# Six 512-column matmuls put ahead of the third tile in three node stages of a four-layer graph network kernel

## The chip, the cores and the metric

The kernel runs as one program on one core of a Trainium2 chip. The metric is the device time of an execution in microseconds, the median of several runs. A core has five engines with instruction streams of their own: TensorE (PE in the rows, its weight loads PEld), VectorE (DVE), ScalarE (ACT), GpSimd (POOL) and SyncE (SP, which here only issues DMAs). They wait for one another through semaphores. TensorE has two clock levels, 2.4 and 1.2 GHz; the profile calls the granted share of full speed PEclk, 1.00 and 0.50.

## The reference

The network has 6250 nodes with 160 features each (64 scalars, 32 vectors of three components) and 100000 edges, sorted by their destination node. Four layers each normalise the nodes, map them, gather rows by the edges' source, multiply by edge weights, sum the messages at the destination and map the sums. What matters here:

```python
h = jnp.maximum(_layernorm(x, axis=-1), 0.0)
# layer 0, nodes: self map and source map, times a node attribute
out_s = xs @ Ws * (a / np.sqrt(xs.shape[1]))[:, None]
out_v = jnp.einsum('nuc,uw->nwc', xv, Wv) * (a / np.sqrt(xv.shape[1]))[:, None, None]
# layer 3, nodes: two source maps and two self maps, each times an attribute
s_s, s_v = (ssa + ssc, sva + svc)
x1s, x1v = (l1a_s + l1c_s, l1a_v + l1c_v)
# layer 2, the end: message sums to nodes, four heads
agg = jax.ops.segment_sum(alpha * h, dst, num_segments=n)
out = node + jnp.concatenate([agg_s @ Wps,
      jnp.einsum('ncx,cd->ndx', agg_v, Wpv).reshape(n, CV * 3)], axis=-1)
```

## The kernel before, in words

The nodes stay in SBUF in x, as 49 tiles of 128 nodes by 160 features, in float32. For this input the kernel takes the path `streamed()` (L2481). Its stages follow one another, most of them with a barrier between: the setup; the node pass of layer 0 (L2514); the edge streams of layers 0 and 1, which hold the node passes of layers 1 and 2 in their tails; the attention pass, the softmax and the gathering of the messages of layer 2 (L2269); `post_l2` (L2359), which maps the sums of messages to nodes; the node pass of layer 3 (L2470); and the edge stream of layer 3, which ends with the store. The change touches the node pass as it is called for layers 0 and 3, and `post_l2`. The branch `general()` calls them too, and isn't taken here.

`node_pass` (L351) first computes the normalisation of all tiles on VectorE, with one square root on ScalarE. Then each of the 49 tiles goes through ScalarE (L434: scale, bias and relu into `tile`), TensorE (L458 and L459: two transposes into the bank `ps_t`), ScalarE (L443, L444: copies to `tile_T`), TensorE (L464: the map of the 64 scalars, L465: the map of the 96 vector components; a float32 matmul appears as two instructions) and VectorE (`finish_l0`, L500 to L503, or `finish_l3`, L520 to L530). SyncE stores the rows for the edge stream (L406). TensorE's order is written by hand: in its step i it transposes tile i and then maps tile i-1. It waits for `copied` before a transpose, for `tile_ready` before a map, and for `fin` of the tile two before the one that it maps, since each of `ps_t`, `ps_s` and `ps_v` has two banks; six of the eight banks are in use. Layer 0 maps to 128 scalar and 192 vector columns, layer 3 to 256 and 384, and its `finish_l3` has eight instructions where `finish_l0` has four.

`post_l2` has one map for each tile: ScalarE copies 84 rows of sums (L2405), TensorE multiplies them with two blocks of 322 columns (L2417, four instructions of 84 rows in all), and VectorE adds a small constant to the denominators (L2445), takes reciprocals (L2447) and adds four products to the tile (L2453). It has four slots of two banks, so all eight banks are in use.

`steps` (L70) writes the first few steps of a stage out one by one (i is then a Python integer) and the others as a loop whose waits and addresses come from registers.

`warm_up(bank)` (L533) issues six matmuls of the identity with the first 512 columns of x into a bank that nobody reads. Four places call it before the change (L637, L906, L1909, L2314): in the edge streams, in the attention pass and in the gathering of the messages, each at the fifth step of the stage.

Of the kernel before, what the change touches and what calls it, by code (L numbers as in the profile page):

```python
# [22 lines left out]
P = 128  # L23
# [22 lines left out]
def build(nc, A, out):  # L46
# [9 lines left out]
    def at_least(eng, sem, value):  # L56

        if isinstance(value, int) and value <= 0:
            return
        eng.wait_ge(sem, value)  # L60
# [9 lines left out]
    def steps(eng, n, lag, emit, warm=4, unroll=2):  # L70


        for i in range(warm):
            emit(i, i % unroll, i // unroll)
        turns = (n - warm) // unroll
        with eng.Fori(0, turns) as j:
            for k in range(unroll):
                emit(j * unroll + (warm + k), (warm + k) % unroll, j + (warm + k) // unroll)
        for i in range(warm + turns * unroll, n + lag):
            emit(i, i % unroll, i // unroll)  # L80

    def live(i, n):
        return not isinstance(i, int) or 0 <= i < n

    def back(s, r, lag, unroll=2):

        return (s - lag) % unroll, r + (s - lag) // unroll
# [16 lines left out]
    def sbuf(ctx, name, shape, dt=F32):  # L104
        return ctx.enter_context(nc.sbuf_tensor(side[0] + name, shape, dt))

    def psum(ctx, name, shape):
        return ctx.enter_context(nc.psum_tensor(side[0] + name, shape, F32))
# [3 lines left out]
    def sem(ctx, name):  # L112
        layer_sems.append(nc.alloc_semaphore(side[0] + name))
        return layer_sems[-1]
# [20 lines left out]
    with whole:  # L135
        x = sbuf(whole, "x", [P, NT * FEAT])
        y4 = sbuf(whole, "y4", [P, NG * TG * 4])
        sums_T = sbuf(whole, "sums_T", [P, 4 * COLS])
        dst_rel = sbuf(whole, "dst_rel", [P, NG * TG])
# [5 lines left out]
        ident = sbuf(whole, "ident", [P, P])  # L145
# [205 lines left out]
        def node_pass(tag, scalar_maps, vector_maps, tables, finish, n_fin, coefs=(), gamma=None):  # L351
# [6 lines left out]
            with ExitStack() as ctx:  # L358
# [9 lines left out]
                ps_t = [psum(ctx, f"{tag}_ps_t{s}", [P, 512]) for s in range(2)]  # L368
                ps_s = [psum(ctx, f"{tag}_ps_s{s}", [P, 512]) for s in range(2)]
                ps_v = [psum(ctx, f"{tag}_ps_v{s}", [P, 512]) for s in range(2)]  # L370
                zeroed = sem(ctx, f"{tag}_zeroed")
                cleared = sem(ctx, f"{tag}_cleared")
                w_loaded = sem(ctx, f"{tag}_w_loaded")
# [11 lines left out]
                with nc.Block() as block:  # L385

                    @block.sync
                    def _(sp):
                        for n, w in enumerate(scalar_maps):
                            sp.dma_start(w_s[:, n * SC:(n + 1) * SC], A[w]).then_inc(w_loaded, 16)  # L390
                        sp.wait_ge(zeroed, 1)

                        for n, w in enumerate(vector_maps):
                            for c in range(XYZ):
                                at = n * VF + c * VC
                                sp.dma_start(w_v[c:VF:XYZ, at:at + VC], A[w]).then_inc(w_loaded, 16)
                        if gamma:
                            sp.dma_start(gam[0:SC, 0:1], A[gamma[0]]).then_inc(w_loaded, 16)
                            sp.dma_start(gam[0:SC, 1:2], A[gamma[1]]).then_inc(w_loaded, 16)
                            for c in range(XYZ):  # L400
                                sp.dma_start(gam[c:VF:XYZ, 2:3], A[gamma[2]]).then_inc(w_loaded, 16)

                        def store(i, s, r):
                            sp.wait_ge(fin, (i + 1) * n_fin)
                            for k in range(n_tab):
                                sp.dma_start(tables[k][ds(i * P, P), :], rows[s][k][:, :]).then_inc(stored[s], 16)  # L406

                        steps(sp, NT, 0, store, unroll=U)
                        for s in range(U):
                            sp.wait_ge(stored[s], 16 * n_tab * len(range(s, NT, U)))  # L410
                        sp.wait_ge(cleared, 1)
# [36 lines left out]
                    @block.tensor  # L448
                    def _(pe):
                        pe.wait_ge(w_loaded, 16 * n_w)  # L450
                        if gamma:
                            pe.wait_ge(w_ready, 1)

                        def step(i, s, r):
                            if live(i, NT):
                                at_least(pe, copied, (i + 1) * (2 if gamma else 1))
                                at_least(pe, tile_ready, 2 * (i - 1))
                                nc.tensor.transpose(ps_t[s][0:VF, P:2 * P], tile[s][:, SC:FEAT], ident[:, :])  # L458
                                nc.tensor.transpose(ps_t[s][0:SC, 0:P], tile[s][:, 0:SC], ident[:, :]).then_inc(turned, 1)  # L459
                            if live(i - 1, NT):  # L460
                                s1, _ = back(s, r, 1)
                                at_least(pe, tile_ready, 2 * i)
                                at_least(pe, fin, (i - 2) * n_fin)
                                nc.tensor.matmul(ps_s[s1][:, 0:ns], tile_T[s1][0:SC, 0:P], w_s[:, :])  # L464
                                nc.tensor.matmul(ps_v[s1][:, 0:nv], tile_T[s1][0:VF, P:2 * P], w_v[:, :]).then_inc(mapped, 1)  # L465

                        steps(pe, NT, 1, step)
# [62 lines left out]
            nc.vector.scalar_tensor_tensor(xv_at(t), by_component(ps_v[:, 3 * VF:4 * VF]), c1, xv_at(t),  # L530
                                           ALU.mult, ALU.add).then_inc(fin, 1)

        def warm_up(bank):  # L533


            for _ in range(6):
                nc.tensor.matmul(bank[:, 0:512], ident[:, :], x[:, 0:512])  # L537


        def edge_pass(tag, first, rows_of, edge_T, w_in, w_mid, w_out, act_fn, scales):  # L540
# [1818 lines left out]
        def post_l2():  # L2359
# [5 lines left out]
            with ExitStack() as ctx:  # L2365
# [6 lines left out]
                ps = [psum(ctx, f"l2_post_ps{s}", [P, 2, 512]) for s in range(U)]  # L2372
# [10 lines left out]
                with nc.Block() as block:  # L2383

                    @block.sync
                    def _(sp):
                        sp.wait_ge(zeroed, 1)
                        for b in range(2):
                            for k in range(2):
                                h, at = 2 * b + k, k * HF  # L2390
                                sp.dma_start(w_all[at:at + HS, b, 0:SC], A["L2_gnn_Wps"][h * HS:(h + 1) * HS, :]).then_inc(w_loaded, 16)
                                for c in range(XYZ):
                                    lo = at + HS + c * HV
                                    sp.dma_start(w_all[lo:lo + HV, b, SC + c * VC:SC + (c + 1) * VC],
                                                 A["L2_gnn_Wpv"][h * HV:(h + 1) * HV, :]).then_inc(w_loaded, 16)
# [13 lines left out]
                    @block.tensor  # L2409
                    def _(pe):  # L2410
                        pe.wait_ge(w_made, 12)

                        def step(i, s, r):
                            at_least(pe, copied, i + 1)
                            at_least(pe, fin, (i - 3) * 4)
                            for b in range(2):
                                ins = nc.tensor.matmul(ps[s][:, b, 0:2 * FEAT + 2], sums[s][:, b, :], w[:, b, :])  # L2417
                            ins.then_inc(mapped, 1)

                        steps(pe, NT, 0, step, unroll=U)  # L2420
# [49 lines left out]
        def layer_3_nodes():  # L2470
            import math
            c_self = math.sin(math.pi / 8)
            node_pass("l3", ["L3_gnn_Ws_l1_a", "L3_gnn_Ws_l1_c", "L3_gnn_Ws_sc_a", "L3_gnn_Ws_sc_c"],
                      ["L3_gnn_Wv_l1_a", "L3_gnn_Wv_l1_c", "L3_gnn_Wv_sc_a", "L3_gnn_Wv_sc_c"], [table[4]], finish_l3, 8,
                      [(0, 1.0), (1, 1.0), (0, c_self), (1, c_self)])
# [17 lines left out]
        def general():  # L2493

            all_windows(EDGE_WIN, lambda tag, first: edge_pass(tag + "l0", first, *L0))
            post_l0()
            node_pass("l1", ["L1_gnn_W1_s", "L1_gnn_W_sc_s"], ["L1_gnn_W1_v", "L1_gnn_W_sc_v"], [table[1], self_rows], finish_l1, 4,
                      [(0, SC ** -0.5), (0, VC ** -0.5)])
            all_windows(EDGE_WIN, lambda tag, first: edge_pass(tag + "l1", first, *L1))
            post_l1()  # L2500
            node_pass("l2", ["L2_gnn_Ws_src", "L2_gnn_Ws_dst"], ["L2_gnn_Wv_src", "L2_gnn_Wv_dst"], [table[2], table[3]], finish_l2, 4,
                      gamma=("L2_gnn_gamma_s", "L2_gnn_beta_s", "L2_gnn_gamma_v"))
            attention_pass()
            softmax_pass()
            spread_exps()
            all_windows(SUM_WIN, gather_messages)
            post_l2()
            layer_3_nodes()
            all_windows(EDGE_WIN, lambda tag, first: edge_pass(tag + "l3", first, *L3))
            post_l3()  # L2510
            store_x()
# [67 lines left out]
```

## Time and profile before

| | us |
|---|---|
| median of 3 runs | 7133.47 (7131.9 to 7139.69) |
| the profiled execution's span | 7132.6 |
| PE busy | 6597.2 (92%) |
| DVE busy | 4139.3 (58%) |
| POOL busy | 4496.1 (63%) |
| layer 0's node pass, from its first transpose | 58.9 to about 162 |
| `post_l2`, from its first matmul | 5621.6 to about 5732 |
| layer 3's node pass, from its first transpose | 5756.0 to about 5913 |

The span is one execution from the first to the last instruction, taken by the profiler; it lies within 1 us of the median. Busy is the time in which an engine worked; the end of a matmul is modelled, and matmuls overlap in the array, so a PE that is busy throughout can still be at half its clock or at work that fills it poorly. PEclk in a row of stretches is the mean granted share. The three stages together are some 370 us of the span.

### The profile page before, as it was taken

To read this page: it belongs to the slowest core of one execution; us is meant where nothing else is said; L and a number is where in the kernel's file an instruction comes from. 1 tells how busy PE (TensorE), PEld (TensorE's weight loads), DVE (VectorE), ACT (ScalarE), POOL (GpSimd) and SP (SyncE) were. 2 spreads that over 40 slices of the span, in tenths; PEclk is the share of its full clock that TensorE was granted. 3 is DMA by queue.
4 is the path that set the end of the run, shared out by engine and by line. 5 is a ranking of instruction groups with operands and counts; after the bars stand their busy time and mean duration, and the time that the engine had idled before them with its cause. 6 is when DMAs were issued, how large, how long until landed. Compare 5 with 4: busy or idle time off the path is not lost. (4 is left out here: it accounts for less than half of the span.)

```text
span 7132.6 us, 185025 instructions
## 1 busy us (share of the span) xinstructions
PE 6597.2 (92%) x57917; PEld 5320.6 (75%) x57917; DVE 4139.3 (58%) x11420; ACT 2382.5 (33%) x6454; POOL 4496.1 (63%) x4226
## 2 busy tenths in 40 slices
PE   6999999899999969999999999999838889999999
PEld 3788888677877757887787787777727636878787
DVE  4555555344444447777777777777658863333333
ACT  2122222112112136666666666666500021111111
POOL 1677777577777757788788878878500015666665
PEclk9999999899999978899889889888869758999999
DMA  1444444354445434444444444444337303444443
GB/s 60 114 121 125 122 123 125 97 131 124 127 125 130 126 66 79 79 83 83 81 81 85 81 82 83 81 81 83 78 91 203 90 19 102 116 117 115 114 117 97
DMA packets 810369, 719.46 MB, mean 101 GB/s; under 512 B 248938, under 2 KB 682074, under 8 KB 809602
## 3 DMA queue, kind: packets, MB, share of 16 engines
q0 software_dynamic: 263424, 321.38, 22.4%
q1 hardware_dynamic: 546818, 396.43, 19.8%
q8 instruction: 75, 1.23, 0.1%
q14 instruction: 52, 0.43, 0.0%
HBM read 557.59 MB, written 159.75 MB: 101 GB/s over the span
## 5 line engine op out<-in xcount | busy, mean ns | idle before, releaser
L892 POOL DMA_INDIRECT l_edge_g<-node_table,l_edge_idx x2352 | 2271.0, 966 | 1292.7 <-issue 937.9
L939 PEld LDWEIGHTS l_edge_win_ps<-l_edge_hot,l_edge_prod 128*128 128x128 f32 (+2 forms) x14112 | 1309.6, 149 | 212.2 <-issue 171.3
L939 PE MATMUL l_edge_win_ps<-l_edge_hot,l_edge_prod 128*128 128x40 f32 (+2 forms) x14112 | 1438.3, 255 | 29.8 <-DVE sums_T L752 22.0
L1857 POOL DMA_INDIRECT att_g<-node_table,att_ends x784 | 1241.1, 1583 | 238.8 <-issue 238.8
L957 ACT ACTIVATE l_edge_h<-l_edge_h_ps 128x256 f32<-128x256 f32 (+1 forms) x784 | 342.8, 437 | 2755.0 <-PE l_edge_h_ps L913 2540.9
L1850 POOL DMA_INDIRECT att_g<-node_table,att_ends x784 | 791.4, 1009 | 301.4 <-issue 272.8
L993 DVE TENSOR_TENSOR l_edge_prod<-l_edge_w_ps,l_edge_g 128x512 f32<-128x512 f32 x588 | 405.6, 690 | 958.0 <-PE l_edge_w_ps L920 810.3
L1877 PE MATMUL att_turn<-ident,sums_T 128*128 128x128 f32 (+1 forms) x4704 | 774.4, 309 | 29.7 <-ACT sums_T L1962 23.2
L1962 ACT ACTIVATE sums_T<-att_turn 128x512 f32<-128x512 f32 (+1 forms) x1176 | 666.1, 592 | 214.6 <-PE att_turn L1877 206.9
L1877 PEld LDWEIGHTS att_turn<-ident,sums_T 128*128 128x128 f32 (+1 forms) x4704 | 572.2, 153 | 204.7 <-issue 120.3
L920 PEld LDWEIGHTS l_edge_w_ps<-l_edge_wo,l_edge_h 64*128 64x128 f32 (+1 forms) x4704 | 503.4, 190 | 287.6 <-issue 285.2
L752 DVE TENSOR_TENSOR sums_T<-sums_T,l_edge_win_ps 128x160 f32 x588 | 189.2, 322 | 878.7 <-PE l_edge_win_ps L943 705.8
L920 PE MATMUL l_edge_w_ps<-l_edge_wo,l_edge_h 64*128 64x192 f32 (+1 forms) x4704 | 679.7, 351 | 0.0
L943 PE MATMUL l_edge_win_ps<-l_edge_hot,l_edge_prod 128*32 128x40 f32 x14112 | 620.6, 204 | 0.0
L997 DVE TENSOR_TENSOR l_edge_prod<-l_edge_w_ps,l_edge_g 128x384 f32<-128x384 f32 x1176 | 594.5, 547 | 0.0
L943 PEld LDWEIGHTS l_edge_win_ps<-l_edge_hot,l_edge_prod 128*32 128x32 f32 x14112 | 568.2, 115 | 0.0
L913 PE MATMUL l_edge_h_ps<-l_edge_ea,l_edge_wi 16*128 16x256 f32 (+1 forms) x1176 | 497.3, 503 | 51.4 <-DMA l_edge_ea<-in_edge_attr_T 49.5
L1934 PEld LDWEIGHTS att_o<-att_w_o1v,sums_T 128*128 128x128 f32 x1568 | 287.9, 216 | 109.9 <-issue 92.8
L1952 ACT ACTIVATE att_gy<-att_g,y 128x160 f32<-128x160 f32 x784 | 270.2, 416 | 252.6 <-DMA att_g<-node_table,att_ends 252.4
L1917 PE MATMUL att_o<-att_w_o2s,sums_T 96*128 96x64 f32 x1568 | 333.7, 297 | 10.7 <-ACT sums_T L1962 1.5
L1935 PE MATMUL att_o<-att_w_o1v,sums_T 128*128 128x64 f32 x1568 | 338.7, 302 | 0.0
L1919 PE MATMUL att_o<-att_w_o2v,sums_T 128*128 128x64 f32 x1568 | 329.6, 295 | 0.0
(271 smaller groups left out, 10179.5 us busy)
## 6 DMA issues: line engine op xcount, KB each, us to landing
l_edge_hot<-hot_tiles SPq DMA_DIRECT2D x392, 320.0 KB
hot_tiles<-l_edge_hot SPq DMA_DIRECT2D x196, 320.0 KB, 2.3
l_messages<-att_rows SPq DMA_DIRECT2D x196, 320.0 KB
sum_msg<-l_messages SPq DMA_DIRECT2D x196, 320.0 KB, 3.6
l_edge_g<-node_table,l_edge_idx POOLq DMA_INDIRECT x2352
att_g<-node_table,att_ends POOLq DMA_INDIRECT x1568
att_ea<-in_edge_attr_T SPq DMA_DIRECT2D x196, 64.0 KB
l_scores<-att_score SPq DMA_DIRECT2D x784, 2.0 KB
```

What stands on the lines that cost most here:

```text
L892: pool.indirect_dma_start(g[s][:, t, :], None, rows_of, bass.IndirectOffsetOnAxis(idx[s][:, t:t + 1], 0)).then_inc(fetched[s], 16)
L913: nc.tensor.matmul(h_ps[0:HALVES * hid, 0:HC], wi[:, :], ea[s0][:, :]).then_inc(hidden[0], 1)
L920: ins = nc.tensor.matmul(w_ps[s1][:, m * (TG // HALVES) + n, 0:wn], h[last][s1][m * hid:(m + 1) * hid, n * P:(n + 1) * P], wo[m * hid:(m + ...
L939: nc.tensor.matmul(at, q[:, t, lo:lo + width], to[:, t, kinds, :], start=t == 0, stop=t == TG - 1)
L943: ins = nc.tensor.matmul(win[SC:MID, 2 * W:3 * W], q[:, t, lo:lo + VC], to[:, t, 1 + c, :], start=c + t == 0, stop=c + t == XYZ + TG - 2)
L957: nc.scalar.activation(h[n][s % 2][:, :], h_ps[0:HALVES * hid, 0:HC], act_fn, scale=scales[n]).then_inc(active[n], 1)
L993: nc.vector.tensor_tensor(halves[:, :, :, 0:SC], w[:, :, 0:2 * SC].rearrange("p t (n f) -> p t n f", n=2), rows[:, :, 0:SC].unsqueeze(2).t ...
L997: ins = nc.vector.tensor_tensor(q[:, :, lo:lo + VF].rearrange("p t (c u) -> p t c u", c=XYZ), w[:, :, VS + n * VC:VS + (n + 1) * VC].unsqu ...
L1850: pool.indirect_dma_start(g[s][:, t, :], None, table[2], bass.IndirectOffsetOnAxis(ends[s][:, t:t + 1], 0)).then_inc(fetched[s], 16)
L1857: pool.indirect_dma_start(g[s1][:, t, :], None, table[3], bass.IndirectOffsetOnAxis(ends[s1][:, TG + t:TG + t + 1], 0), compute_op=ALU.add ...
L1877: ins = nc.tensor.transpose(turn[bank][0:width, t * P:(t + 1) * P], f[:, t, at:at + width], ident[:, :])
L1962: nc.scalar.activation(feat_T[n][0:width, part, :], turn[bank][0:width, :], ACT.Copy).then_inc(count, 1)
```

## The change

At the third tile (i == 2, which is in the steps written out) TensorE first issues the six matmuls, and then its instructions of that step. In the node pass they go into a seventh bank, `spare_ps`, allocated for them; in `post_l2` into the first bank of slot 3, before that slot's first real matmul, which overwrites it. The 512 moving columns come from `dst_rel`, which is constant after the setup, and no longer from x, which VectorE is writing at that point. No wait, no DMA and no instruction of another engine is added or moved, and the four earlier calls stay as they were.

```diff
+                spare_ps = psum(ctx, f"{tag}_spare_ps", [P, 512])
...
                         def step(i, s, r):
+                            if isinstance(i, int) and i == 2:
+                                warm_up(spare_ps, dst_rel)
                             if live(i, NT):
...
-        def warm_up(bank):
+        def warm_up(bank, moving=x):
             for _ in range(6):
-                nc.tensor.matmul(bank[:, 0:512], ident[:, :], x[:, 0:512])
+                nc.tensor.matmul(bank[:, 0:512], ident[:, :], moving[:, 0:512])
...
                         def step(i, s, r):
+                            if isinstance(i, int) and i == 2:
+                                warm_up(ps[3][:, 0, :], dst_rel)
                             at_least(pe, copied, i + 1)
```

## Rows read from the trace of the kernel before

**Rows 1.** The page: TensorE's granted clock in 40 slices of the span, in tenths.

```profile
PEclk9999999899999978899889889888869758999999
```

**Rows 2.** Stretches: length, busy time (instructions) of each engine, PEclk, DMA share, GB/s.

```profile
58.00:162.00 104.00, 102.52 (x294) 66.48 (x294) 46.45 (x195) 43.65 (x147) 0.00 (x0) 1.00 0.12 37
5622.00:5727.00 105.00, 105.00 (x196) 65.50 (x195) 84.48 (x281) 18.76 (x45) 0.00 (x0) 0.50 0.00 0
5756.00:5912.00 156.00, 154.79 (x294) 67.29 (x294) 92.70 (x389) 43.02 (x146) 0.00 (x0) 0.50 0.08 25
```

**Rows 3.** Groups of the two node passes: count, busy us, mean ns, idle before.

```profile
L458 PE MATMUL l_ps_t<-ident,l_tile 128*96 128x128 f32 x49 | 20.6, 421 | 37.9 <-ACT l_tile L434 37.9
...
L458 PE MATMUL l_ps_t<-ident,l_tile 128*96 128x128 f32 x49 | 20.6, 421 | 28.9 <-ACT l_tile L434 28.9
```

**Rows 4.** A stretch of the attention pass, and its transposes of 128 columns.

```profile
2833.00:2840.50 7.50, 5.70 (x47) 5.06 (x45) 4.56 (x16) 3.49 (x10) 5.98 (x6) 1.00 0.51 90
...
L1877 PE MATMUL att_turn<-ident,sums_T 128*128 128x128 f32 x8 | 1.0, 273 | 0.0
```

**Rows 5.** Timeline of layer 0's node pass: start us, length, engine, instruction, idle before.

```profile
63.93 0.28 DVE L500 TENSOR_SCALAR l_rows<-l_ps_s,l_coef 128x64 f32<-128x64 f32 x1 [1.03 <-PE l_ps_v L465]
64.25 0.79 PE L464 MATMUL l_ps_s<-l_w_s,l_tile_T 64*128 64x128 f32 x2
64.55 0.33 DVE L503 SCALAR_TENSOR_TENSOR x<-l_ps_v,l_coef,x 128x96 f32<-128x96 f32 x1
66.33 0.79 PE L464 MATMUL l_ps_s<-l_w_s,l_tile_T 64*128 64x128 f32 x2
```

**Rows 6.** Timeline of layer 3's node pass, within the loop.

```profile
5769.79 1.22 PE L464 MATMUL l_ps_s<-l_w_s,l_tile_T 64*128 64x256 f32 x2
...
5772.94 0.28 DVE L520 TENSOR_SCALAR l_temp<-l_ps_s,l_coef 128x64 f32<-128x64 f32 x1 [1.52 <-PE l_ps_v L465]
5772.94 1.22 PE L464 MATMUL l_ps_s<-l_w_s,l_tile_T 64*128 64x256 f32 x2
5773.05 0.27 ACT L443 ACTIVATE l_tile_T<-l_ps_t 64x128 f32<-64x128 f32 x1 [2.23 <-PE l_ps_t L459]
5773.59 0.52 ACT L434 ACTIVATE l_tile<-x,norm 128x160 f32 x1
5774.04 0.28 DVE L526 SCALAR_TENSOR_TENSOR l_rows<-l_ps_s,l_coef,l_temp 128x64 f32<-128x64 f32 x1 [0.15 <-DVE x L523]
5774.66 0.34 DVE L530 SCALAR_TENSOR_TENSOR x<-l_ps_v,l_coef,x 128x96 f32 x1
```

**Rows 7.** Timeline of `post_l2`: its start, its third tile on VectorE, and its end.

```profile
5621.57 4.66 PE L2417 MATMUL l_post_ps<-l_post_w,l_post_sums 84*128 84x322 f32 x8 [9.89 <-DVE l_post_w L2440]
...
5628.42 0.16 DVE L2445 TENSOR_SCALAR l_post_inv<-l_post_ps 128x4 f32<-128x4 f32 x1
...
5718.33 8.79 PE L2417 MATMUL l_post_ps<-l_post_w,l_post_sums 84*128 84x322 f32 x16
...
5727.57 0.15 DVE L2445 TENSOR_SCALAR l_post_inv<-l_post_ps 128x4 f32<-128x4 f32 x1
...
5729.73 0.15 DVE L2445 TENSOR_SCALAR l_post_inv<-l_post_ps 128x4 f32<-128x4 f32 x1
```

**Rows 8.** Instructions of L537 in the gathering of the messages: duration min/median/max, first and last start.

```profile
L537 PE MATMUL sum_spare_ps<-x,ident x12: 592/592/648, 5295.6 to 5300.4; 128*128 128x512 f32 x12
```

**Rows 9.** Stretches as in rows 2: the gathering of the messages, from its start.

```profile
5285.00:5290.00 5.00, 0.31 (x3) 0.34 (x3) 1.68 (x5) 0.00 (x0) 3.18 (x1) 0.50 0.00 0
5290.00:5295.00 5.00, 5.00 (x40) 5.00 (x40) 2.76 (x9) 0.00 (x0) 0.00 (x0) 0.53 0.53 135
5295.00:5300.00 5.00, 5.00 (x22) 2.61 (x21) 2.35 (x7) 0.00 (x0) 0.00 (x0) 1.00 0.69 186
5300.00:5610.00 310.00, 268.48 (x3075) 244.80 (x3073) 276.30 (x764) 0.00 (x0) 0.00 (x0) 1.00 0.75 198
```

**Rows 10.** Stretches as in rows 2: the edge stream of layer 0 around a drop.

```profile
400.00:403.40 3.40, 1.99 (x16) 1.76 (x15) 1.83 (x4) 1.70 (x4) 2.49 (x4) 1.00 0.54 154
403.40:406.80 3.40, 3.40 (x40) 3.00 (x37) 0.00 (x0) 0.00 (x0) 2.48 (x4) 0.50 0.30 71
```

## The prediction, made before the changed kernel was run

> **What bounds the kernel now.** I read the page's clock line first [rows 1]. TensorE is at nine tenths of full clock or more over most of the span and lowest around slice 32, where `post_l2` and layer 3's node pass lie. The stretches [rows 2] say it sharply: `post_l2` runs 105 us and layer 3's node pass 156 us at a granted 0.50, the 1.2 GHz level, though PE is busy for 105.00 and 154.79 us of them. So in these stages TensorE isn't starved: it works all the time at half clock.
>
> For layer 0's node pass the same view prints 1.00. I don't believe it. The groups [rows 3] give the 128-column transpose L458 421 ns in layer 0 and 421 ns in layer 3, where the clock is 0.50; the 128-column transpose L1877 in a stretch at 1.00 takes 273 ns [rows 4]. Equal forms with equal durations have equal clocks, so layer 0's pass is at 1.2 GHz too, and its printed 1.00 is a clock that no record covers. The only term of mine that rests on this is layer 0's.
>
> Next, who waits for whom. In layer 0 a tile takes 66.33-64.25=2.08 us on PE, and VectorE starts its tile after 1.03 us of waiting for L465 [rows 5]. In layer 3 a tile takes 5772.94-5769.79=3.15 us, with waits of 1.52 us by VectorE and 2.23 us by ScalarE, both for PE [rows 6]. PE sets the pace of both passes. `post_l2` is different: PE's last matmul ends at 5718.33+8.79=5727.12, and VectorE still has two tiles to do; it starts them 5729.73-5727.57=2.16 us apart with nothing left to wait for. From its third tile to the last it took (5729.73-5628.42)/46=2.20 us a tile, while PE produced one each 2.15 us (5727.12-5621.57=105.55 us for 49). VectorE is the bound there, by a hair [rows 7].
>
> **The block by itself.** Six float32 matmuls are twelve instructions. At 1.00 the last of twelve starts 4.8 us after the first and lasts 0.59 [rows 8], about 5.3 us in all. That is the lower end, if the clock were up from the start. At 1.2 GHz all the way it would be near twice that, 10.5 us: the upper end. Between them: in the gathering of the messages PE goes from idle to busy at about 5290 and the clock is up some 5 us later: the mean of 0.53 in 5290 to 5295 leaves 0.3 us at 1.00 [rows 9]. With 5 us at half speed 2.5 us of full-speed work are done, and 5.3-2.5=2.8 remain: 7.8 us a block. PE has nothing else to do meanwhile, and everybody waits for it.
>
> Will the block raise the clock at all? No row shows that: the twelve of rows 8 ran at full level already, and so did the others of L537, by their 592 ns. For it: the bursts after which the clock rose had 128-row matmuls back to back [rows 9], as the block has. The node passes and `post_l2` have matmuls of 64, 96 and 84 rows, and stay at 0.50 however busy they are [rows 2].
>
> The Trainium skill has a rule that speaks against the change's need (TensorE: Matmul & The Clock Gate, "Why this matters for your kernels"): keep TensorE continuously busy and it is granted its full clock. By that rule `post_l2`, busy 105.00 us of 105.00, would be at 1.00, all three stages would be fast already, and the change would only add three blocks, about 16 us. The row says 0.50 [rows 2], so the measurement decides against the rule here: how long PE is busy is not enough, and what it is busy with counts.
>
> **Layer 0's node pass.** 47 tiles follow the block. At full clock, PE needs at least half of 2.08, 1.04 us, and at most 2.08*273/421=1.35 us, if everything shrinks only as the whole transpose does [rows 3, 4]. VectorE needs 64.55+0.33-63.93=0.95 us [rows 5] plus the 0.15 us that an own completion costs it in the loop [rows 6], 1.10. ScalarE needs 5773.59+0.52-5773.05=1.06 us [rows 6], and again up to 0.15. All three come close together; I take 1.20 us, near the middle. The gain is 47*(2.08-1.20)=41.4 us (34 to 49), the block costs 7.8, and the net is -34 us, if the clock stays up. PE would then be at work nearly all the time, so I take it that it does.
>
> **Layer 3's node pass.** PE would need 3.15/2=1.58 us at least, 3.15*273/421=2.04 at most. VectorE needs 5774.66+0.34-5772.94=2.06 us and 0.15 for its wait for itself: 2.21 us [rows 6]. So VectorE becomes the bound, and PE then idles in every tile. The gain is at most 47*(3.15-2.21)=44 us, less 7.8: -36 us. But does the clock stay? The nearest rows: the edge stream lost its 1.00 right behind a stretch in which PE was busy for 1.99 of 3.40 us, and the gathering kept it for 310 us with 268 us busy, all in 128-row matmuls [rows 9, 10]. Layer 3's PE would be busy about 1.6 to 2.0 of 2.21 us, in 64- and 96-row matmuls for three quarters of it. That lies between, and nearer to the loser: I expect the clock to fall back after roughly a quarter of the tiles, 12. Then the gain is 12*0.94=11 us, and with the block -3 us; range +8 to -36.
>
> **`post_l2`.** VectorE already runs at its own pace of 2.16 to 2.20 us, so a faster PE brings nothing. The block starts when PE is done with tile 1, about 5625.9 (4 x 1.07 us behind 5621.57), and ends at 5633.7; tile 2's matmuls take 1.1 us at full clock, so VectorE starts that tile near 5634.9 and not at 5628.42: +6.5 us. At the block's ends: +4 and, as VectorE's lag at the end absorbs some, +8.
>
> The Trainium skill states for holding the clock that gaps between bursts of matmuls are what loses it (same page, "HAM oscillation — how this bites in real kernels"). Layer 3's PE would have only short gaps, so by that rule the clock would stay up: that is the first rival below. Rows 10 agree that waiting loses it, but show no gap that long beforehand.
>
> Nothing else moves: no DMA, no wait and no other engine's instruction is added, and each stage ends in a barrier, before which PE idles anyhow. Sum: -34-3+6.5=-31 us on the profiled 7132.6, thus about 7102; the median is 0.9 us above the span: 7102.5.
>
> **The rivals.** (1) The clock rises and stays in both node passes: -34-36+6.5=-63.5, 7070 us. For it: short gaps only. Against it: PE idles a fifth of the time or more, in low-row matmuls. (2) Slower: the blocks run, but the passes can't hold the level, or it never rises. The block is PE's only new work, and it's exposed in all three places: 7.8+7.8+6.5=+22 if the clock drops right behind each, 10.5+10.5+8=+29 if it never rises: 7155 to 7162. For it: the passes' own matmuls stay at 0.50 for 100 us and more [rows 2], and no row shows a block that lifted anything. It decides once fewer than some 9 tiles of layer 0 (7.8/0.88) run at full clock. (3) Both passes lose the level on the way: layer 0 halfway (-21+8=-13), layer 3 soon (+2), `post_l2` +6.5: 7129 us, within the noise at the edge. (4) Layer 0's printed 1.00 is true; then its block is pure loss, 5.3 us, and the sum is near +9: 7142. The 421 ns speak against that.
>
> **How the numbers follow.** Forecast 0.42, rival 1 0.24, rival 2 0.17, rival 3 0.12, rival 4 0.05. What a measurement can tell from no change is about 0.2%, 14 us. Forecast and rival 1 are faster: 0.66, and a third of rival 3 lands beyond 14 us: 0.70. The rest of rival 3 and most of rival 4 are the same: 0.12. Slower is rival 2 and the remainder: 0.18. The forecast's own range, from its pace bounds (1.10 to 1.35 us in layer 0: -5, +7) and from layer 3's +8 to -20, is 7080 to 7121. Eight in ten must take in rival 1 and the near end of rival 2: 7062 to 7155.
>
> **What would show it.** In the changed trace: twelve instructions of L537 near 62 us, 5626 us and 5760 us, each block 7 to 9 us long, the later ones of a block at 592 ns; L458 at about 270 ns behind the block in layer 0, with tiles 1.1 to 1.3 us apart; granted 1.00 in the first 20 to 40 us behind the block of layer 3, L520 starting each 2.2 us there, and 3.15 us apart once the clock is back at 0.50; in `post_l2` the same 2.16 to 2.20 us a tile on VectorE, whatever the clock. The prediction is wrong if L458 stays at 421 ns in layer 0, if layer 3's whole pass stays at 1.00, or if `post_l2` gets shorter.

## The result, and the profile after

The changed kernel takes 7091.07 us, the median of 6 runs (7077.21 to 7106.26), against 7132.68 (7118.78 to 7139.69) for the kernel before. The ratio is 0.9945, with a 95% interval of 0.9928 to 0.9963. A second measurement of the same pair gave 0.9950 (0.9928 to 0.9972). So it is faster by about half a per cent, 39 to 42 us, where 31 were forecast. One profile used below, that of the kernel without a block in `post_l2`, is of an execution in the slow state; what is read from its stages stands in other runs too.

The profiled execution of the changed kernel has a span of 7081.9 us, 50.7 under that of before, more than the medians differ by. Cutting both traces at the first and the last instruction of each stage shows where this lies:

| us | before | changed | difference | forecast |
|---|---|---|---|---|
| layer 0's node pass, first transpose to last update | 103.6 | 67.0 | -36.6 | -34 |
| edge streams of layers 0 and 1 | 2400.1 | 2399.3 | -0.8 | 0 |
| attention pass and softmax | 2727.0 | 2708.8 | -18.2 | 0 |
| gathering of the messages | 331.9 | 332.2 | +0.3 | 0 |
| `post_l2`, first matmul to last update | 110.2 | 115.8 | +5.6 | +6.5 |
| layer 3's node pass | 156.9 | 154.8 | -2.1 | -3 |
| edge stream of layer 3 | 1219.7 | 1220.6 | +0.9 | 0 |

The three stages that the change touches give -33.1 us. The other large entry, the attention pass, has the same code in both kernels; the experiments come back to it. The table leaves out the 24 us between `post_l2` and layer 3's first transpose, which are equal in both.

First the blocks. Instructions of L540 (L537 before) in the changed kernel; columns as in [rows 8]:

```profile
L540 PE MATMUL l_spare_ps<-dst_rel,ident x24: 592/592/1061, 61.8 to 5717.1; 128*128 128x512 f32 x24
L540 PE MATMUL sum_spare_ps<-x,ident x12: 592/592/648, 5240.6 to 5245.4; 128*128 128x512 f32 x12
L540 PE MATMUL l_post_ps<-dst_rel,ident x12: 592/592/1061, 5570.9 to 5577.5; 128*128 128x512 f32 x12
```

The new blocks begin at 1061 ns an instruction and end at 592, where the old block in the gathering never was slower than 648: the new ones meet the engine at its lower level and lift it. The timeline of layer 0's block and what follows:

```profile
61.77 7.18 PE L540 MATMUL l_spare_ps<-dst_rel,ident 128*128 128x512 f32 x12
...
65.19 0.34 PEld L540 LDWEIGHTS l_spare_ps<-dst_rel,ident 128*128 128x128 f32 x1 [0.52 <-issue]
65.79 0.19 PEld L540 LDWEIGHTS l_spare_ps<-dst_rel,ident 128*128 128x128 f32 x1 [0.27 <-issue]
...
70.15 0.28 DVE L503 TENSOR_SCALAR l_rows<-l_ps_s,l_coef 128x64 f32<-128x64 f32 x1 [7.08 <-PE l_ps_v L468]
71.31 0.28 DVE L503 TENSOR_SCALAR l_rows<-l_ps_s,l_coef 128x64 f32<-128x64 f32 x1 [0.20 <-PE l_ps_v L468]
72.47 0.28 DVE L503 TENSOR_SCALAR l_rows<-l_ps_s,l_coef 128x64 f32<-128x64 f32 x1 [0.20 <-PE l_ps_v L468]
```

The weight loads fall from 0.34 to 0.19 us at about 65.5, some 3.8 us into the block. VectorE waits 7.08 us for it, and then works a tile each 1.16 us instead of 2.08 [rows 5], with 0.20 of waiting left. The transposes behind the block, against 421 ns in [rows 3]:

```profile
L461 PE MATMUL l_ps_t<-ident,l_tile 128*96 128x128 f32 x47 | 12.9, 274 | 0.0
```

The granted clock in stretches, with columns as in [rows 2]. The first is layer 0 behind the rise. The next three are `post_l2` ahead of its rise, at full level, and afterwards, and the last three are the same for layer 3.

```profile
65.50:126.00 60.50, 59.32 (x294) 39.56 (x293) 45.87 (x192) 41.12 (x139) 0.00 (x0) 1.00 0.21 62
5570.90:5574.60 3.70, 3.70 (x6) 1.59 (x5) 2.08 (x7) 0.42 (x1) 0.00 (x0) 0.50 0.00 0
5574.60:5588.30 13.70, 12.08 (x39) 6.90 (x39) 7.69 (x27) 2.91 (x7) 0.00 (x0) 1.00 0.00 0
5588.30:5676.00 87.70, 87.34 (x159) 46.10 (x157) 71.77 (x239) 14.99 (x36) 0.00 (x0) 0.50 0.00 0
5710.20:5714.60 4.40, 4.40 (x7) 1.76 (x6) 1.91 (x8) 0.00 (x0) 0.00 (x0) 0.50 0.06 19
5714.60:5735.10 20.50, 17.90 (x60) 8.28 (x58) 14.01 (x59) 8.05 (x27) 0.00 (x0) 1.00 0.08 24
5735.10:5859.00 123.90, 123.90 (x235) 53.89 (x234) 75.77 (x318) 33.04 (x113) 0.00 (x0) 0.50 0.09 26
```

Layer 0 keeps 1.00 to its end. `post_l2` loses it after 13.7 us and layer 3 after 20.5 us. Layer 3's timeline around the loss, against [rows 6]:

```profile
5731.45 0.27 PE L461 MATMUL l_ps_t<-ident,l_tile 128*96 128x128 f32 x1
5732.28 0.70 PE L467 MATMUL l_ps_s<-l_w_s,l_tile_T 64*128 64x256 f32 x2 [0.44 <-DVE x L533]
5733.65 0.28 PE L461 MATMUL l_ps_t<-ident,l_tile 128*96 128x128 f32 x1
5734.48 0.70 PE L467 MATMUL l_ps_s<-l_w_s,l_tile_T 64*128 64x256 f32 x2 [0.44 <-DVE x L533]
5736.54 0.42 PE L461 MATMUL l_ps_t<-ident,l_tile 128*96 128x128 f32 x1
5737.11 1.22 PE L467 MATMUL l_ps_s<-l_w_s,l_tile_T 64*128 64x256 f32 x2
```

Before it PE waits 0.44 us a tile for VectorE (L533), with tiles 2.20 us apart; behind it the matmuls are long again and VectorE waits for PE. Right behind the block, while VectorE was still catching up, the first tiles were 1.69 us apart. And `post_l2`'s end, against [rows 7]:

```profile
5669.52 6.94 PE L2422 MATMUL l_post_ps<-l_post_w,l_post_sums 84*128 84x322 f32 x12
...
5673.74 0.15 DVE L2450 TENSOR_SCALAR l_post_inv<-l_post_ps 128x4 f32<-128x4 f32 x1
5675.90 0.15 DVE L2450 TENSOR_SCALAR l_post_inv<-l_post_ps 128x4 f32<-128x4 f32 x1
5678.06 0.15 DVE L2450 TENSOR_SCALAR l_post_inv<-l_post_ps 128x4 f32<-128x4 f32 x1
5680.22 0.15 DVE L2450 TENSOR_SCALAR l_post_inv<-l_post_ps 128x4 f32<-128x4 f32 x1
```

VectorE's tiles are 2.16 us apart as before, with PE two tiles ahead.

### The profile page after: what moved, and what is told of

It reads as the page before. It is cut to its first block and busy times, and to the rows that moved or that the text cites. A ratio compares the mean times of both kernels' runs of the same rounds, so it can differ in the third digit from the quotient of the medians.

```text
span 7081.9 us, 185097 instructions
## 1 busy us (share of the span) xinstructions
PE 6533.2 (92%) x57953; PEld 5266.3 (74%) x57953; DVE 4141.2 (58%) x11420; ACT 2379.8 (34%) x6454; POOL 4494.5 (63%) x4226
## 5 line engine op out<-in xcount | busy, mean ns | idle before, releaser
L1938 PE MATMUL att_o<-att_w_o1v,sums_T 128*128 128x64 f32 x1568 | 339.3, 302 | 0.0
L1920 PE MATMUL att_o<-att_w_o2s,sums_T 96*128 96x64 f32 x1568 | 329.1, 294 | 10.7 <-ACT sums_T L1965 1.5
L1937 PE MATMUL att_o<-att_w_o1v,sums_T 128*128 128x64 f32 x1568 | 326.1, 293 | 0.0
```

The source lines that it names most:

```text
L1937: nc.tensor.matmul(o1[:, t, Q:PV + VC], feat_T[0][:, 1, e], w_o1v[0][:, :])
```

## The experiments

The first four were measured in a series of measurements in which the kernel before takes 9442.66 us (median of 23 runs) and not 7133. The edge streams of layers 0 and 1 take 3544 us there against 2400, and the attention pass about 3400 against 2727. In the stages studied here unchanged code takes the same time in both (`post_l2` 110.3 and 110.2 us, layer 3's pass 156.9 and 156.9), so these runs are read by their stages. Why the other stages are slower is open. It isn't shown to be the chip: this series and a later one, in which the kernel before takes 7151, carry the same chip number. Of all runs below only the first two and the last two have several executions behind their totals; the others are one execution each, and only their stages are read.

**Only layer 0's block.**

```diff
-                            if isinstance(i, int) and i == 2:
+                            if isinstance(i, int) and i == 2 and tag == "l0":
                                 warm_up(spare_ps, dst_rel)
...
-                            if isinstance(i, int) and i == 2:
-                                warm_up(ps[3][:, 0, :], dst_rel)
```

> Only layer 0's block stays. My theory (each stage's gain is its own): layer 0's pass, from its first transpose to the end of its last update, takes 67 us instead of 103, `post_l2` 110 and layer 3's pass 157 us as before the change; the whole is 36 us under the kernel before, near 7096. Rival (the three blocks together do something for the stages between, where the changed kernel's profile is 18 us shorter than I can account for): the middle, from layer 0's pass to `post_l2`, comes back to the 5459 us of before and the gain is under 36 us.

Measured: layer 0's pass 67.8 us, `post_l2` 110.3, layer 3's pass 156.9. Each block acts on its own stage alone. The whole is 0.9986 of the kernel before (0.9948 to 1.0023): in this series the other stages vary too much for 36 us to be seen in the total, so the rival on the middle stays open here.

**No block in `post_l2`.** The second half of the diff above.

> The blocks of layers 0 and 3 stay, that of `post_l2` goes. My theory (`post_l2` is bound by VectorE, so its block only costs): `post_l2` back from 115.8 to 110.2 us, layers 0 and 3 at 67 and about 155 us, the whole 5 to 6 us under the changed kernel, near 7086. Rival (a faster PE does help `post_l2`): it stays at 116 us or gets longer than 110, and the whole is no better than the changed kernel.

Measured: 66.3, 110.3 and 155.7 us; 0.9951 of the kernel before (0.9914 to 0.9987). `post_l2` is back at its old length, as in the five later runs without its block (110.2 to 110.3 us). The block cost 5.5 us and gave nothing.

**Blocks of 64 rows.**

```diff
-                nc.tensor.matmul(bank[:, 0:512], ident[:, :], moving[:, 0:512])
+                nc.tensor.matmul(bank[:, 0:512], ident[0:rows, :], moving[0:rows, 0:512])
```

with rows=64 in the three new calls (`rows` is a new argument, 128 by default).

> The three blocks use only 64 rows of the identity and of the moving tile, the same number of instructions and columns. Theory A (what PE is busy with counts, and low-row matmuls don't lift the clock): the granted clock stays at 0.50 in all three stages, each block takes about 10.3 us, layer 0's pass 114 us, layer 3's 167, `post_l2` 118 to 120, some 29 us over the kernel before. Rival (long dense columns count, whatever their rows): blocks of about 7 us and layer 0's pass at 67 us as in the changed kernel.

Measured: 114.3, 121.1 and 167.6 us in the three stages, each 10.7 to 10.9 us over the kernel before (a little more than expected in `post_l2`). The rows of its blocks:

```profile
L540 PE MATMUL l_spare_ps<-dst_rel,ident x24: 1057/1057/1219, 61.9 to 7561.1; 64*128 64x512 f32 x24
L540 PE MATMUL l_post_ps<-dst_rel,ident x12: 1057/1057/1219, 7406.9 to 7416.4; 64*128 64x512 f32 x12
```

None is faster than 1057 ns. The same instructions and columns, at the same pace to begin with, lift the clock with 128 rows and don't with 64. This is rival 2 of the prediction made to happen; it is the rows that keep the change from it. Each row of the identity brings one non-zero weight, and no run separates the number of rows from that of such weights.

**Blocks of three matmuls.** `warm_up(..., 3)` in the three new calls.

> Three matmuls (six instructions) a block instead of six, 5.1 us at half clock. In the changed kernel the clock rose 3.7 to 4.3 us into each block, at its fifth or sixth instruction. Theory (the first half of the block does the lifting, the rest only costs): the clock rises in layer 0 and layer 3, layer 0's pass takes about 64.5 us. Rival (where the block falls against the chip's own timing decides, and a short one can miss): at least one of the three stages stays at 0.50 throughout, layer 0's pass then at 108 us.

Measured: 64.8, 112.7 and 147.7 us. The clock rose in all three stages, and each block cost less: in `post_l2` 2.4 us instead of 5.5. Layer 3 kept it 27.3 us this time, which is part of its gain. The rival isn't excluded by this: in layer 0 the clock rose 4.3 us into a block of 4.9, and in other runs with long blocks up to 5.4 us into one. In the five stages with a short block it rose each time.

The next five ran in series in which the kernel before takes 7151 us (one run) and 7132 (median of 14).

**A 128-row matmul in every tile of layer 3.** No block in `post_l2`, and behind the transposes of the node pass:

```diff
+                                if tag in ("l3",) and not (isinstance(i, int) and i < 2):
+                                    nc.tensor.matmul(spare_ps[:, 0:192], ident[0:128, :], dst_rel[0:128, 0:192])
```

> Blocks in layers 0 and 3 (none in `post_l2`), and in every tile of layer 3's pass one more unread matmul between its transposes and its maps, 192 columns with 128 rows of the identity. Theory (the clock fell in layer 3 because PE, waiting for VectorE, did too little in its rows; more rows at work hold it): 1.00 to the end of the pass, tiles at VectorE's 2.2 us, the pass about 115 us instead of 155 to 157. Rival (the clock is held only for a time after a block, whatever follows; layer 0 just ended in time, 61 us after the rise): it falls after 20 to 60 us, and the tiles then cost 3.15+0.8 us, the pass 150 us or more.

Measured: layer 3's pass takes 117.5 us, with its clock up to the end of its matmuls.

**The same with 32 rows.** `ident[0:32, :], dst_rel[0:32, 0:192]`.

> As the run before, but the added matmul of each tile takes only 32 rows of the identity, with the same columns and so the same time on PE. Theory A (rows at work count): hardly more than none, the clock falls within some 10 to 30 us of the rise, and the pass gets longer than the 157 us of the kernel before, about 175 to 185. Theory B (idle gaps of PE count, rows don't): the gaps are filled as with 128 rows, the clock stays, about 115 us.

Measured: 118.4 us, with the clock up until 0.8 us before the end of the last matmul. My theory A as I had put it failed: 32 rows are enough. That left two readings, that rows count and little was missing, or that only PE's gaps or columns count. The run with a single row tells them apart.

**The same with one row.** `ident[0:1, :], dst_rel[0:1, 0:192]`.

> As the two runs with an added matmul per tile in layer 3, with a single row of the identity: the same columns and the same time on PE, and next to nothing in its rows. Theory A (rows at work count; 32 of them were just enough): the clock falls within 10 to 40 us of the rise and the pass takes about 175 to 185 us. Theory B (PE's idle gaps or its moving columns count, rows don't): 1.00 to the end and 117 to 119 us, as with 32 and 128 rows.

Measured: the clock falls 13.7 us after its rise, as theory A says, and the pass takes 198.9 us, longer than its 175 to 185. The stretches behind the blocks, first with 128 rows:

```profile
5730.40:5837.00 106.60, 98.53 (x376) 53.08 (x376) 91.70 (x384) 40.81 (x138) 0.00 (x0) 0.99 0.12 36
```

With 32 rows:

```profile
5707.30:5815.00 107.70, 104.74 (x376) 52.76 (x376) 91.75 (x384) 40.57 (x137) 0.00 (x0) 0.98 0.12 36
```

With one row, ahead of the fall and after it:

```profile
5741.40:5751.00 9.60, 9.60 (x36) 4.90 (x35) 6.49 (x28) 4.21 (x15) 0.00 (x0) 1.00 0.08 26
5751.00:5925.00 174.00, 174.00 (x341) 79.73 (x340) 81.66 (x343) 36.86 (x125) 0.00 (x0) 0.50 0.07 20
```

(The 0.99 and 0.98 come from the last microseconds, as the pass ends.) The one-row run has PE busy for 9.60 of 9.60 us and loses the clock; with 128 rows PE is busy for 98.53 of 106.60 and keeps it. Busy time doesn't order these runs, rows do. The cleanest pair is 32 rows against one: with both, tiles are 2.20 to 2.21 us apart at full level and the added matmul has the same columns. At 0.50 a tile then costs 4.09 us, the 3.15 of before and 0.94 for the added matmul, so this filler costs most where it fails: 42 us over the kernel before in this stage.

**Less work on VectorE in layer 3.** `finish_l3` without its four updates of x, so that the self maps are missing from the output; no block in `post_l2`. `finish_l3` then increments `fin` four times a tile and not eight, and the call says so (not shown).

```diff
-            nc.vector.scalar_tensor_tensor(xs_at(t), ps_s[:, 2 * SC:3 * SC], c0, xs_at(t), ALU.mult, ALU.add).then_inc(fin, 1)
...
-            dve.wait_ge(fin, k + 4)
+            dve.wait_ge(fin, k + 2)
```

> Blocks in layers 0 and 3; `finish_l3` leaves out its four additions to x (the self maps of layer 3 are missing from the output), so VectorE needs 1.2 to 1.4 us a tile and no longer 2.2. Theory (VectorE's pace makes PE idle and so loses the clock): PE is the bound at the 1.69 us a tile that it had right behind the block, 1.00 to the end, the pass about 91 us. Rival (64- and 96-row matmuls can't hold it in layer 3 whatever the pace): the clock falls as in the changed kernel and the pass takes over 140 us.

Measured: 92.5 us, tiles 1.69 us apart throughout, and in its stretch:

```profile
5723.80:5805.00 81.20, 80.43 (x284) 39.16 (x283) 48.49 (x191) 40.97 (x139) 0.00 (x0) 1.00 0.15 47
```

The same 64- and 96-row matmuls hold the clock when VectorE doesn't thin them out. So in the changed kernel layer 3 lost its clock because its matmuls came each 2.2 us and not each 1.7.

**The clock held in `post_l2`.** The changed kernel with, ahead of each tile's maps:

```diff
+                            if not (isinstance(i, int) and i < 3):
+                                nc.tensor.matmul(ps[s][:, 0, 0:192], ident[:, :], dst_rel[:, 0:192])
```

> The changed kernel with one more unread 128-row matmul of 192 columns ahead of each tile's maps in `post_l2`, so that the clock is held there. Theory (VectorE bounds `post_l2`): 1.00 to the end of the stage and still 115 to 116 us, VectorE's tiles 2.16 to 2.20 us apart. Rival (PE's pace matters): with the clock up the stage falls below the 110 us of the kernel before.

Measured: 116.0 us. The stretch and the maps in it:

```profile
5615.00:5714.00 99.00, 78.62 (x282) 48.75 (x280) 79.71 (x266) 17.92 (x43) 0.00 (x0) 0.98 0.00 0
```

```profile
L2424 PE MATMUL l_post_ps<-l_post_w,l_post_sums 84*128 84x322 f32 x172 | 54.9, 441 | 0.0
```

The maps take 441 ns instead of 742, the clock is up for nearly the whole stage, and its length is what it was with the block alone. (The 0.98 holds one fall of 3.4 us, at 5643.) VectorE is the bound of `post_l2` at either level.

**The version these point to, and the changed kernel beside it.** Blocks of three matmuls in layers 0 and 3, none in `post_l2`, and in each tile of layer 3 `nc.tensor.matmul(spare_ps[:, 0:64], ident[:, :], dst_rel[:, 0:64])`.

> What the runs so far point to: blocks of three matmuls in layers 0 and 3, none in `post_l2`, and in layer 3 one unread 128-row matmul of 64 columns a tile. Expected: layer 0's pass 65 us, `post_l2` 110, layer 3's pass 113 to 116 with 1.00 to its end; together 81 us under the kernel before, near 7052, and about 40 us under the changed kernel. Rival (64 columns are too few, or the short block misses the lift in one of the passes): layer 3's pass over 145 us, and no more than 50 us under the kernel before.

> The changed kernel again, beside the version above. Stage by stage as before: 67, 115.8 and about 155 us; the whole 33 us under the kernel before (the sum of the three stages), if the further 18 us that its first profile showed in the attention pass are spread of that pass and not of the change. Rival (the change shortens the attention pass too): 45 to 55 us under the kernel before.

Measured, on the same chip: the new version 7052.64 us (median of 6), 0.9883 of the kernel before (0.9856 to 0.9910), with 64.8, 110.3 and 114.0 us in the three stages, in sum 81.6 under before. The changed kernel 7093.57 (median of 9), 0.9950, with 66.2, 115.8 and 154.7, in sum 34.0 under. Both totals follow from their stages within their intervals. Layer 3 in the new version:

```profile
5718.00:5824.00 106.00, 91.16 (x376) 52.89 (x374) 91.70 (x384) 40.61 (x137) 0.00 (x0) 1.00 0.12 36
```

**The attention pass.** Its code is the same in all kernels. In the profiles outside the slower series it took 2727.0 (before), 2708.8 (changed) and, in the order of the runs above, with the changed kernel's second profile last, 2730.4, 2706.8, 2728.4, 2719.2, 2742.5, 2708.1 and 2712.8 us. Its stretches in before, in the changed kernel, and in the longest one:

```profile
2562.60:5289.60 2727.00, 2460.39 (x17679) 2047.29 (x17679) 1957.67 (x5520) 1636.20 (x4536) 2043.31 (x1570) 0.85 0.41 79
```

```profile
2525.40:5234.20 2708.80, 2435.32 (x17679) 2024.84 (x17679) 1957.78 (x5520) 1633.67 (x4536) 2043.39 (x1570) 0.86 0.41 80
```

```profile
2529.00:5271.00 2742.00, 2477.03 (x17679) 2059.94 (x17679) 1959.04 (x5518) 1634.98 (x4536) 2049.68 (x1570) 0.84 0.41 79
```

In these three it is longer where less clock was granted; over all nine that holds only roughly. Kernels that contain the change had both nearly the shortest and the longest. I take the 18.2 us of the first pair for this spread. It isn't shown: there is only one such profile of the kernel before, and the interval of the second measurement reaches 51 us, 17 more than its stages give, so that a part of the 18 us may still belong to the change.

## Why the prediction was right, point by point

- **Layer 0 ran at 1.2 GHz in spite of its printed 1.00: right.** Equal forms had 421 ns before and 274 behind the block. The changed trace prints 1.00 for its first microseconds too, where L540 takes 1061 ns.
- **The block lifts the clock: right,** which no row of before showed. The reason given, 128-row matmuls, was the right one: 64 rows don't.
- **The block's price: 7.8 us forecast, 7.1 of waiting measured in layer 0.** The rise came 3.7 to 4.3 us into the block in this trace. Over all runs in which a block lifted the clock it came 1.6 to 5.4 us into it, so that the forecast's 5 lies inside, and a block of six took between 6.3 and 8.0 us.
- **Layer 0's pace: 1.20 forecast, 1.16 to 1.17 measured,** and with the price above this makes some -36 of the measured -36.6, for a forecast of -34. That the clock stays up was forecast from PE being at work nearly all the time. It did stay, but the one-row run shows that busy time alone doesn't hold it, so the reason given was incomplete.
- **Layer 3's pace at full level: 2.21 forecast, 2.20 measured,** VectorE being the bound. The fall after a quarter of the tiles, 12: it came after nine at full level, and -3 became -2.1. The 12 was placed between two rows and not computed, and in the five layer 3 passes with a block and nothing added the level lasted 17 to 27 us, so how near it came is in part luck. What I had weighed was mainly PE's idling; the run with one row shows that idling is not the measure and that the rows in use count. In the changed kernel the two go together, so the forecast held for a reason that was only half named.
- **`post_l2`: +6.5 forecast, +5.6 measured,** and bound by VectorE with the clock held as well.
- **Rival 1** (the clock stays in both passes) would have come true with one 32-row matmul of 192 columns more a tile, or with less work on VectorE: the forecast was right by a small margin, and 0.24 was not too much for it. The Trainium skill's rule that gaps are what loses the clock (TensorE: Matmul & The Clock Gate, "HAM oscillation — how this bites in real kernels") is not borne out by the one-row run, where PE was busy for 9.60 of 9.60 us ahead of the fall.
- **What was left out:** the sum took the rest of the kernel as fixed. The attention pass alone spreads by 36 us between single executions, from 2706.8 to 2742.5. Of the 39 to 42 us of the medians the three stages explain 33 to 34; the rest is within the intervals and its cause isn't shown.

## What to carry to other kernels

A stage in which TensorE sets the pace and is granted half its clock, although it is busy throughout, can be lifted by a few dense full-row matmuls that nobody reads; check first that no other engine's pace lies just below, since then the block only costs (here 5.6 us). In every lift seen here the clock rose while the block still ran, at most 5.4 us into it; whether a block that ends sooner lifts it isn't shown. Holding the clock is a question apart from raising it: where another engine becomes the bound, a small full-row matmul in each tile, put where TensorE would wait anyway, held it and, with the shorter block, turned 2 us of gain into 43. Compare durations of equal instruction forms before believing a granted clock at the start of a trace.

## What the runs showed of the hardware that was not expected

- Rows, not busy time: a block of 64 rows stayed at 1057 ns for all its twelve instructions, where one of 128 rows went from 1061 to 592 within 3.7 to 4.3 us (1.6 to 5.4 over all runs); an added matmul of one row left the clock to fall after 13.7 us, one of 32 rows in the same place held it to within 0.8 us of the last matmul's end.
- `post_l2` kept PE busy for 87.34 of 87.70 us at 0.50 behind its loss, and nothing in it ever raised the clock again.
- Two series of measurements agree on the node stages to tenths (110.2 and 110.3 us, 156.9 and 156.9) and differ by half in the edge streams of layers 0 and 1 (2400 and 3544 us); the cause is open.
